# A token pipeline whose first and last steps are written out, each engine in its own order

## The reference, cut to what matters

```python
h = _layernorm(x, axis=-1) * (1 + ca) + sa
x = x + ga * _L0_attn_ref(h, L0_attn_qkv, L0_attn_wo)
h = _layernorm(x, axis=-1) * (1 + cb) + sb
x = x + gb * _L0_ffn_ref(h, L0_ffn_W_r, L0_ffn_W_k, L0_ffn_W_v, L0_ffn_mu_r, L0_ffn_mu_k)
...
x = x + ga * _L1_attn_ref(h, L1_attn_Wq, L1_attn_Wk, L1_attn_Wv, L1_attn_Wbeta, L1_attn_b_beta, L1_attn_Wo, L1_attn_b_o, L1_attn_ln_g, L1_attn_ln_b)
h = _layernorm(x, axis=-1) * (1 + cb) + sb
x = x + gb * _L1_ffn_ref(h, L1_ffn_router_w, L1_ffn_router_b, L1_ffn_w_gate, L1_ffn_w_up, L1_ffn_w_down, L1_ffn_sw_gate, L1_ffn_sw_up, L1_ffn_sw_down)
```

## Time and profile before

| | us |
|---|---|
| median of 3 runs (2132.54 to 2135.54) | 2133.79 |
| the profiled execution, its own time | 2135.56 |
| its span, first to last instruction | 2133.8 |
| PE busy | 1937.6 (91%) |
| DVE busy | 1710.2 (80%) |
| ACT busy | 1422.5 (67%) |
| POOL busy | 952.4 (45%) |

### The profile page before, as it was taken

How to read it: one execution, slowest core, us unless ns; L and a number is a source line. 1 busy time by engine, 2 the same in 40 slices (tenths; PEclk the granted TensorE clock), 3 DMA queues, 4 the chain that set the end, 5 groups by cost and what they waited for, 6 DMA issues and landing times. The chain is left out here.

```text
span 2133.8 us, 30293 instructions
## 1 busy us (share of the span) xinstructions
PE 1937.6 (91%) x10299; PEld 834.4 (39%) x10427; DVE 1710.2 (80%) x2497; ACT 1422.5 (67%) x1921; POOL 952.4 (45%) x825
## 2 busy tenths in 40 slices
PE   7889999988999989999899899799999887999997
PEld 4442222222222222222222222466666544777775
DVE  6779999999999999999999999667888864333332
ACT  5768999989899988999899999546445421111110
POOL 4864454443334433444433344244776652433434
PEclk9999999999999999999999999999999988999999
DMA  6652120222212021117130000210001023544541
GB/s 209 198 172 45 32 46 1 33 48 45 33 23 33 13 57 23 33 23 200 59 95 26 13 23 23 66 40 20 31 31 40 32 71 103 107 111 96 123 103 25
DMA packets 123391, 133.74 MB, mean 63 GB/s; under 512 B 33753, under 2 KB 117554, under 8 KB 122544
## 3 DMA queue, kind: packets, MB, share of 16 engines
q1 hardware_dynamic: 108656, 117.86, 20.7%
q0 software_dynamic: 14592, 14.08, 3.7%
HBM read 96.85 MB, written 50.63 MB: 69 GB/s over the span
## 5 line engine op out<-in xcount | busy, mean ns | idle before, releaser
L1383 DVE SCALAR_TENSOR_TENSOR arena<-ps_s,arena 128x1024 f32<-128x1024 f32 (+1 forms) x1071 | 1147.0, 1138 | 45.6 <-ACT arena L1343 37.5
L1343 ACT ACTIVATE arena<-ps_s 128x1024 f32<-128x1024 f32 (+1 forms) x1194 | 1041.3, 934 | 113.1 <-PE ps_s L1278 99.9
L1278 PE MATMUL ps_s<-arena 128*128 128x512 bf16 (+3 forms) x2176 | 581.6, 365 | 104.0 <-DVE arena L1383 76.8
L1294 PE MATMUL ps_o<-arena,values 128*32 128x512 f32 (+3 forms) x4608 | 565.9, 568 | 9.4 <-ACT arena L1330 4.3
L1397 POOL TENSOR_SCALAR arena<-arena 128x512 f32<-128x512 f32 x123 | 236.4, 1922 | 498.7 <-ACT arena L1348 498.6
L1278 PEld LDWEIGHTS ps_s<-arena 128*128 128x128 bf16 x2304 | 155.2, 97 | 695.2 <-DVE arena L1383 530.9
L1973 ACT ACTIVATE arena<-t_ps_four 128x320 f32<-128x320 f32 (+1 forms) x96 | 42.0, 438 | 302.5 <-PE t_ps_four L1842 302.5
L2311 POOL DMA_INDIRECT out<-values,slot_ids x80 | 123.6, 1545 | 222.0 <-DVE values L2222 195.0
L1842 PE MATMUL t_ps_four<-arena 128*128 128x320 f32 (+1 forms) x768 | 214.7, 436 | 0.6 <-DVE arena L2181 0.6
L1294 PEld LDWEIGHTS ps_o<-arena,values 128*32 128x32 f32 x4608 | 94.0, 108 | 233.0 <-issue 185.5
L2194 DVE TENSOR_TENSOR arena<-t_ps_four,arena 128x320 f32<-128x320 f32 (+1 forms) x96 | 47.2, 492 | 167.1 <-ACT arena L1973 167.1
(11 more groups left out here) (207 smaller groups left out, 1772.2 us busy)
## 6 DMA issues: line engine op xcount, KB each, us to landing
arena<-parts_dram SPq DMA_DIRECT2D x320, 64.0 KB, 2.2
parts_dram<-arena SPq DMA_DIRECT2D x32, 384.0 KB, 3.0
arena<-parts_dram SPq DMA_DIRECT2D x24, 512.0 KB, 7.3
slots_in_dram<-in_empty_slots SPq DMA_DIRECT2D x10, 1040.0 KB, 25.7
arena<-slots_in_dram SPq DMA_DIRECT2D x16, 650.0 KB, 4.9
arena<-in_L_ffn_w_gate SPq DMA_DIRECT2D x16, 352.0 KB, 3.2
arena<-in_L_ffn_w_up SPq DMA_DIRECT2D x16, 352.0 KB, 3.8
arena<-in_L_attn_x SPq DMA_DIRECT2D x8, 512.0 KB, 4.3
```

The costliest lines, as they stand in the source:

```text
L1278: last = pe.matmul(ps_s[:, unit.bank + i, p.at:p.at + p.width], m.k_stack[:, group.g % 2 * HG + p.head, p.kt * P:p.kt * P + P], q_stack[:, ...
L1294: last = pe.matmul(ps_o[32 * p.head:32 * p.head + 32, p.w0:p.w0 + p.width], m.values_flat[:, at:at + 32], probs[:, job.at % PROB_BANKS, p. ...
L1343: act.activation(probs[:, unit.slot:unit.slot + n], ps_s[:, unit.bank:unit.bank + n], ACT.Exp, scale=1.0 / DH ** 0.5).then_inc(exped, 1)
L1383: dve.scalar_tensor_tensor(p, ps_s[:, unit.bank:unit.bank + n], 0.0, p, ALU.not_equal, ALU.mult).then_inc(bank, 1)
```

## The change

`staged` now runs steps 3 to 8 alone. The calls of the first three steps and of all steps from 9 on are written out for each engine, in an order that is not that of the lists. No call is added or left out; the calls for block 0 that returned at once are gone, and so are the tests for block 0 in the calls themselves (`constants` of DVE is called once instead). `Uses` gets the order of PE's opening and closing uses as text ("up14" is `up(4, 1)`) and counts in the whole order. Steps 3 to 8 keep their order on all engines. POOL has nothing in steps 0 to 2. The calls before and after, for the same step numbers:

- PE's opening before: `turn_attn(1)`, `turn_attended(0)`, `attend_out(1)`, `turn_attn(2)`, `mix_keys(0)`, `mix_gate(0)`, `mix_value(0)`, `turn_attended(1)`, `turn_mixed(0)`, `attend_out(2)`, `project_narrow(0)`.
- ACT's opening before: `take_attn(1)`, attended 0, `rectify(0)`, `open_gate(0)`, `take_attn(2)`, `normalise_attended(1)`, attended 1, `normalise_mixed(0)`, `modulate_mixed(0)`, `take_narrow(0)` and the rest.
- DVE's opening has the same order as before.

The core of the diff (the written-out lists in the order PE opening, PE closing, ACT opening, ACT closing, DVE opening, DVE closing, POOL closing):

```diff
 BLOCKS = NG * NB
+STEADY = range(3, 9)
...
 class Uses:
 
 
-    def __init__(self, **skews):
-        self.order = list(skews.items())
+    def __init__(self, opening, closing, **skews):
+        def calls(text):
+            return [(call[:-1], int(call[-1])) for call in text.split()]
+
+        steady = [(name, t - skew) for t in STEADY for name, skew in skews.items() if 0 <= t - skew < NB]
+        self.order = calls(opening) + steady + calls(closing)
 
     def before(self, name, b):
-
-        t = b + dict(self.order)[name]
-        n = sum(min(max(t - skew, 0), NB) for _, skew in self.order)
-        for other, skew in self.order:
-            if other == name:
-                return n
-            n += 0 <= t - skew < NB
+        return self.order.index((name, b))
...
     def staged(stages):
-        for t in range(NB + max(skew for skew, _ in stages)):
+        for t in STEADY:
...
-    turns = Uses(attn=0, up1=5, final=4, attended=1, up2=5, mixed=2, up0=4)
-    outs = Uses(gate=2, value=2, count=5, logits=4, delta=3, down=5, attend=0)
-    banks = Uses(keys=2, spread0=3, spread1=3)
+    turns = Uses("attn0 attended0 attn1 attn2 mixed0 attended1",
+                 "up14 final5 up24 mixed7 up05 up15 final6 up25 up06 up16 final7 up26 up07 up17 up27",
+                 attn=0, up1=5, final=4, attended=1, up2=5, mixed=2, up0=4)
+    outs = Uses("attend0 attend1 gate0 value0 attend2",
+                 "gate7 value7 count4 logits5 delta6 down4 count5 logits6 delta7 down5 count6 logits7 down6 count7 down7",
+                 gate=2, value=2, count=5, logits=4, delta=3, down=5, attend=0)
+    banks = Uses("keys0",
+                 "keys7 spread06 spread16 spread07 spread17",
+                 keys=2, spread0=3, spread1=3)
...
             pe.wait_ge(m.weights_in, m.weights_expected)
+            turn_attended(0)
+            turn_attn(1)
+            attend_out(1)
+            mix_keys(0)
+            mix_gate(0)
+            mix_value(0)
+            turn_attn(2)
+            attend_out(2)
+            turn_mixed(0)
+            turn_attended(1)
+            project_narrow(0)
             staged([(0, turn_attn), (2, mix_keys), (3, lambda b: project_keys(b, 0)), (3, lambda b: spread(b, 0)),
...
+            mix_keys(7)
+            project_keys(6, 0)
+            mix_gate(7)
+            spread(6, 0)
+            mix_value(7)
+            up(4, 1)
+            count(4)
+            project_keys(6, 1)
+            spread(6, 1)
+            turn_final(5)
+            up(4, 2)
+            make_logits(5)
+            delta_out(6)
+            turn_mixed(7)
+            project_narrow(7)
+            down(4)
+            spread(7, 0)
+            up(5, 0)
+            project_keys(7, 0)
+            count(5)
+            up(5, 1)
+            project_keys(7, 1)
+            turn_final(6)
+            spread(7, 1)
+            make_logits(6)
+            up(5, 2)
+            delta_out(7)
+            down(5)
+            up(6, 0)
+            up(6, 1)
+            count(6)
+            turn_final(7)
+            make_logits(7)
+            up(6, 2)
+            down(6)
+            count(7)
+            up(7, 0)
+            up(7, 1)
+            up(7, 2)
+            down(7)
...
+            modulate("attended", 0, m.h_even[:, :, 0 * BT + 1:0 * BT + BT + 1], 0, 2, 3)
+            take_attn(1)
+            rectify(0)
+            open_gate(0)
+            normalise_attended(1)
+            take_attn(2)
+            normalise_mixed(0)
+            modulate_mixed(0)
+            modulate("attended", 1, m.h_even[:, :, 1 * BT + 1:1 * BT + BT + 1], 0, 2, 3)
+            take_narrow(0)
+            rectify(1)
+            take_keys(0, 0)
+            open_gate(1)
...
+            open_up(4, 1)
+            normalise_final(5)
+            take_keys(6, 1)
+            modulate("final", 5, m.h_even[:, :, 5 * BT:5 * BT + BT], 1, 2, 3)
+            open_up(4, 2)
+            normalise_mixed(7)
+            exponentials(5)
+            modulate_mixed(7)
+            take_narrow(7)
+            ln_1.normalise(act, 6, rows_of(6), rows_of(6))
+            open_up(5, 0)
+            open_up(5, 1)
+            take_keys(7, 0)
+            take_keys(7, 1)
+            normalise_final(6)
+            modulate("final", 6, m.h_even[:, :, 6 * BT:6 * BT + BT], 1, 2, 3)
+            open_up(5, 2)
+            ln_1.normalise(act, 7, rows_of(7), rows_of(7))
+            open_up(6, 0)
+            exponentials(6)
+            open_up(6, 1)
+            normalise_final(7)
+            modulate("final", 7, m.h_even[:, :, 7 * BT:7 * BT + BT], 1, 2, 3)
+            open_up(6, 2)
+            exponentials(7)
+            open_up(7, 0)
+            open_up(7, 1)
+            open_up(7, 2)
...
+            mix(0)
+            mix_again(0)
+            add_attended(1)
+            constants()
+            combine(0)
+            mix(1)
+            mix_again(1)
...
+            add_shared(3)
+            hide(4, 0)
+            add_delta(5)
+            choose(4)
+            scan(6, 0)
+            combine(7)
+            hide(4, 1)
+            scan(6, 1)
+            find_places(4)
+            take_logits(5)
+            hide(4, 2)
+            residual(6)
+            choose(5)
+            add_shared(4)
+            hide(5, 0)
+            add_delta(6)
+            hide(5, 1)
+            scan(7, 0)
+            find_places(5)
+            scan(7, 1)
+            take_logits(6)
+            hide(5, 2)
+            residual(7)
+            add_shared(5)
+            hide(6, 0)
+            add_delta(7)
+            hide(6, 1)
+            choose(6)
+            find_places(6)
+            take_logits(7)
+            hide(6, 2)
+            choose(7)
+            add_shared(6)
+            find_places(7)
+            hide(7, 0)
+            hide(7, 1)
+            hide(7, 2)
+            add_shared(7)
...
+            difference(6)
+            ln_d.deviation(pool, 5)
+            rows_mixed(5)
+            rows_final(3)
+            ln_1.deviation(pool, 4)
+            gain(4)
+            ln_e.deviation(pool, 4)
+            deviate_attended(7)
+            rows_final(4)
+            ln_d.deviation(pool, 6)
+            rows_mixed(6)
+            difference(7)
+            ln_1.deviation(pool, 5)
+            gain(5)
+            scatter(2)
+            ln_e.deviation(pool, 5)
+            ln_d.deviation(pool, 7)
+            scatter(3)
+            rows_final(5)
+            ln_1.deviation(pool, 6)
+            gain(6)
+            ln_e.deviation(pool, 6)
+            rows_mixed(7)
+            scatter(4)
+            rows_final(6)
+            ln_1.deviation(pool, 7)
+            gain(7)
+            ln_e.deviation(pool, 7)
+            scatter(5)
+            rows_final(7)
+            scatter(6)
+            scatter(7)
```

23 lines of the change are left out of this document (5 added, 18 removed).

## The result

| | before | after |
|---|---|---|
| median of 12 runs, us | 2134.15 | 2130.66 |
| lowest to highest | 2132.43 to 2138.02 | 2126.42 to 2136.34 |
| ratio, 95% interval | | 0.9978 [0.997, 0.9986] |
| the profiled execution, its own time; span | 2135.56; 2133.8 | 2129.72; 2128.0 |

The change gains 3.5 us (two later measurements on other chips gave 6.9 and 10.4), where the forecast had 15 and its range ended at 2125.7. In the profile after `mix_keys` stands at L1728, `rows_out` at L1699, the transposes at L1707, `project_narrow` L1750, `up` L1783, `down` L1797, `make_logits` L1808, `count` L1816, `turn_rows` L1829, the experts' first product L1843.

A forecast was written before the change was run, and what follows sets the result against it. In the last five steps no engine was taken as full: a latency chain through block 7 sets the end. 14.2 us there plus 1.0 from the opening made 15.2, a median of 2119 us, range 2114.5 to 2125.7.

The forecast's parts named there:

- Opening: First steps of the token pipeline: reordered calls bring `mix_keys(1)` 1.0 us earlier, bounds 0 and 2.
- Steps 9 and 10: Up to `delta_out(7)`: earlier `project_narrow(7)` and fewer DVE waits start `delta_out(7)` at 1706.9 instead of 1713.14, 6.2 us earlier.
- The clock stays up: Rival: shorter PE waits before 1732 keep the higher clock, some 4 us more gained in the chain; 2115; chance 0.15.
- Steps 10 and 11: Up to `logits(7)`: normalisation ahead of `open_up(6,0)` puts `logits(7)` at 1734.8 instead of 1741.79; gain so far 7.0 us.
- The middle gives nothing: Rival: a missed wait in steps 9 to 11 loses their 7.0 us; gain 8.2, time 2125.6; chance 0.12.
- Step 12: `exponentials(7)` behind `open_up(6,2)` puts `choose(7)` at 1744.9, before `down(6)`, and `find_places(7)` 14.2 us earlier at 1753.5.
- What was under cover: Behind `find_places(7)`: hides, `up`s, `down(7)` and `add_shared(7)` stay hidden by 1.3 us at full clock; cost taken as 0.
- the prediction's own mark of being wrong: Wrong if the experts' start moves under 9 or over 19 us, or experts wait for `add_shared(7)` rather than their rows.
- The third rival: Slower: tail behind `find_places(7)` at 1.2 GHz takes 30.8 us; with the first rival's 7 lost too, 2136.1; chance 0.03.
- Sum: 14.2 us up to the experts' start plus 1.0 from the opening make 15.2; median 2118.6, rounded to 2119.

The follow-up runs named there:

- b1: Changed kernel with 12 unread matmuls (product never read) put into PE's wait ahead of `turn_final(6)`: 2123.55 us, ratio 0.9941 to the kernel before.
- e1: The changed kernel as it is, measured a third time: 2129.76 us, ratio 0.9956 to the kernel before.
- f1: Changed kernel with the old opening, 6 unread matmuls ahead of `turn_final(6)`, 3 ahead of `logits(6)`, and the early copy: 2117.15 us, ratio 0.992 to before.
- b3: Changed kernel with the early copy alone (first expert's turned rows copied between `add_shared(7)`'s PSUM additions and its rest): 2124.39 us, ratio 0.9941 to before.
- c4: The kernel before with the early copy alone: 2139.76 us, ratio 0.9992 to the kernel before.
- a1: The changed kernel once more, for a second profile: 2132.32 us, ratio 0.9966 to the kernel before.
- d2: Changed kernel with 6 unread matmuls ahead of `turn_final(6)`, 3 ahead of `logits(6)`, and the early copy: 2121.93 us, ratio 0.9921 to before.
- b2: Changed kernel with unread matmuls in later waits: 9 ahead of `up(6,1)`, 24 of `count(6)`, 12 of `up(7,1)`: 2132.74 us, ratio 0.9988 to before.
- b4: Changed kernel with the edits of b1, b2 and b3 together: 2127.88 us, ratio 0.9962 to the kernel before.
- c1: Changed kernel with 6 unread matmuls ahead of `turn_final(6)` and the early copy: 2128.21 us, ratio 0.9942 to the kernel before.
- d1: Changed kernel with 12 unread matmuls ahead of `turn_final(6)` and the early copy: 2125.39 us, ratio 0.9936 to the kernel before.
- a4: The new closing alone, with the old opening: 2132.42 us, ratio 0.9966 to the kernel before.
- c3: As c1, with 5 more unread matmuls ahead of `delta_out(0)` in the opening: 2128.69 us, ratio 0.9942 to the kernel before.
- d3: Changed kernel with `spread(7,1)` ahead of `turn_final(6)` and the early copy, no unread matmuls: 2129.87 us, ratio 0.9955 to before.

## Why the prediction was wrong

Times as distances from `mix_keys(7)`, so that the forecast and the profiles compare (us):

| | before | forecast | after | b1 |
|---|---|---|---|---|
| `project_narrow(7)` | 42.6 | 32.3 | 32.3 | 32.3 |
| `delta_out(7)` | 67.6 | 61.3 | 66.7 | 63.6 |
| `turn_final(7)` | 93.4 | 86.4 | 91.2 | 87.0 |
| `logits(7)` | 96.2 | 89.2 | 94.0 | 89.8 |
| `down(6)` | 106.3 | 99.3 | 104.9 | 99.2 |
| `find_places(7)` | 122.1 | 107.9 | 113.5 | 107.9 |
| first expert matmul | 146.0 | 131.8 | 139.4 | 132.5 |

**Opening: right in kind, small.** 1.0 us was forecast; `mix_keys(1)` comes 26.7 to 27.3 us after `mix_keys(0)` with the new opening and 27.5 to 28.6 with the old, 0.8 between the means, which no median shows. The forecast had nothing for a lower clock ahead of `mix_keys(0)`, where eleven of fifteen profiles lost some 2 us in `attend_out(1)`.

**Steps 9 and 10: the step that failed.** "PE, with `up(5,2)` in between, starts `delta_out(7)` at 1706.9" took DVE's second scan as last and PE as ready for it. The scan ended 2.0 us late (61.8 us behind `mix_keys(7)`, forecast 59.8): a sum scan of `find_places(5)`, L2248, took 2.04 us instead of 0.29, beside a sum of `rows_mixed(7)` on POOL that began 0.11 us ahead of it and ended at 1702.52, 0.15 before the scan; it is so in b1 as well, with 2.05. PE was 5.3 late. The change makes PE's work earlier up to 1697.9 and not the normalised rows that come next, so it turned spread-out idle time into one wait of 2.85 us, and what followed ran at 1.2 GHz. The trace of before has these two calls at 1.93 and 5.35 us, so 1.7 of the 4.2 us could have been read there; the rest is not in that trace; it came with the longer wait. For the clock I had a rival on where it might rise ("The clock stays up"), and none on where it might fall. b1, which takes the waits away, has the forecast's times within 0.7 us from `turn_final(7)` on. In part that is luck: its `delta_out(7)` is still 2.3 us late, and `add_delta(7)` only 1.0, so the forecast's path between the two held some slack that it did not count.

**Steps 10 and 11.** The rival "The middle gives nothing" had these prices: a meeting of POOL and DVE and a low clock in `up(5,2)`. Both came: from b1 to after 3.0 us for the clock, 1.25 net for the meeting (1.67 on DVE, less 0.4 of a wait that b1 had; the trace of before has the same sum at 2.90 us, there beside `rows_final(6)`). Its 8.2 us of gain are near the 6.9 + 0.8 of the closing and the opening below; its chance of 0.12 was too small.

**Step 12: right.** `choose(7)` stands ahead of `down(6)`, and from it to `find_places(7)` it is 8.75 us (forecast 8.6). The exponential again starts 0.01 us behind the table load, so the drain of about 1.38 us that the Trainium skill's page "ScalarE: Activation LUTs", section "What ACT_TABLE_LOAD costs", has beside each load does not show here either. Only the clock is new: `up(6,2)` at 6.58 us where b1 has 5.17, another 1.4 us.

**What was under cover: wrong.** I took 0 with 1.3 us to spare, from `up`s at full clock. `up(7,1)` and `up(7,2)` took 10.12 us instead of 7.1, and the tail cost 2.0. In e1 they took 7.14, and `take` still began 1.32 us behind the first turned rows, where f1 with the early copy has 0.67, so some 0.7 us of cost are left at full clock. That was the prediction's own mark of being wrong, that the experts wait for `add_shared(7)`. b1 to after is 1.3 of it, forecast to b1 0.7. b3 showed it, and c4 that it is new in this order. The third rival had the price of the low clock there (30.8 us from the end of `find_places(7)` to the experts), but read it only against the start of now: from the forecast's own end at 1757.1 it gives 1787.9, 10.5 us past 1777.4, and nothing between 0.6 and that was priced.

**Sum.** The closing lacks 3.0 + 1.25 + 1.4 + 1.3 + 0.7 = 7.65 us of the forecast's 14.2 (139.4 less 131.8 is 7.6). These are differences of single profiles; that the first four come from the clock and the meeting is shown for the stretch up to `delta_out(7)`, and read from rows behind it. Over the profiles, the change's closing is 139.4, 142.4 and 137.8, the old one's 145.8 to 148.2, mean 146.7: 6.9 gained. The middle of the same three is 253.2 to 254.5, and 249.2 to 250.6 in the five with the old closing. Some 4 us of the gain are lost there, the forecast had nothing for it, and it is measured but not explained. 6.9 + 0.8 - 4.0 = 3.7 us. That it is near the 3.5 of the first medians is chance: the same two kernels gave 6.9 (a1) and 10.4 (e1), and the distances take in neither `attend_out(1)` nor the first expert's matmuls.

## What to carry to other kernels

When a reordering packs an engine's work, look for the wait that its idle time gathers into, and price what runs behind it at PE's low clock too, even where the trace of before shows it at the high one. A few unread matmuls in a wait gained some 3 us here (the closing is 136.5 in b3 and 133.2 in d2, with nine of them), where they left the whole stretch to the next long calls free of waits. Their number matters: twelve in a wait of 2.85 us still gained (b1), 24 in one of 6.8 us did not (b2, b4). Measure to the end, not to the first call of the next phase: here that left out nearly half of what the early copy gains. Work that lay under another wait is the next bound once that wait is gone: put the copy that the next phase needs ahead of sums that nobody waits for.

## What the runs showed of the hardware

- Behind a wait of 0.99 us, which followed unread matmuls, transposes and the products of `spread(7,1)`, `up(5,2)` took 6.51 us (c1); without it five profiles (b1, b4, d1, d2, f1) had 3.65. The wait of 2.14 or 2.15 us ahead of `up(6,1)` was followed by the full clock in six profiles and by the low one in four, so the length of one wait does not tell it.
- Which of POOL and DVE pays for a meeting was decided by 0.04 to 0.21 us: 2.90 against 1.23 us on DVE. A small operation pays too: a scan of 0.29 us took 2.04 beside POOL's sum.
- In nine profiles of the new closing (a1, a4, c1 to c3, d1 to d3, e1), not in after, b1 to b4 and f1, the readers of `turn_mixed(7)` were late: in c1 ACT waits 4.82 us, and the profile names the releaser only as "remote" (so do DVE's two waits behind `delta_out(6)`, one call before, 2.28 and 0.70 us); `project_narrow(7)` then waits 3.15 us where b1 has 1.16, and took 3.46 instead of 1.96. These up to 3.5 us stay unexplained. Timeline of c1:

```profile
1685.13 1.45 ACT L1958 ACTIVATE arena<-t_ps_turn,mod_cols 128x512 f32<-128x512 f32 x2 [4.82 <-remote]
1686.63 3.46 PE L1750 MATMUL t_ps_four<-arena 128*96 128x512 f32 x4 [3.15 <-ACT arena L1958]
```
